# Second feed-forward product of eight encoder layers in three float32r passes instead of float32, with the token tensor parked in HBM meanwhile

## What is computed

```python
for i in range(8):
    residual = x
    Q = elu(x @ Wq[i] + bq[i]) + 1          # 16 heads of 64
    Kf = elu(x @ Wk[i] + bk[i]) + 1
    V = x @ Wv[i] + bv[i]
    ...
    y = gelu(att @ Wo[i] + bo[i])
    x = layer_norm(y + residual, ln1_s[i], ln1_b[i])
    residual = x
    h = gelu(x @ W1[i] + b1[i])             # 128 -> 512
    h = gelu(h @ W2[i] + b2[i])             # 512 -> 128: the product that is changed
    x = layer_norm(h + residual, ln2_s[i], ln2_b[i])
```

## Time and profile before

| what | us |
|---|---|
| median of 3 runs (lowest, highest) | 3317.26 (3315.12, 3319.06) |
| profiled execution, its own time | 3315.69 |
| span of that execution in the trace | 3313.6 |
| PE busy in the span | 2981.3 |
| DVE busy | 2659.7 |
| ACT busy | 2443.1 |
| POOL busy | 855.6 |

### The profile page before, as it was taken

The page is one execution under the profiler, slowest core; times in us unless marked ns, Lnnn a source line. Parts: engine busy times, 40 slices in busy tenths (PEclk is TensorE's granted clock), DMA queues, the critical chain, the costliest instruction groups (busy, mean ns, idle before and its releaser), DMA issues. The chain is left out here.

```text
span 3313.6 us, 50990 instructions
## 1 busy us (share of the span) xinstructions
PE 2981.3 (90%) x14368; PEld 1986.3 (60%) x14368; DVE 2659.7 (80%) x10476; ACT 2443.1 (74%) x4542; POOL 855.6 (26%) x1011
## 2 busy tenths in 40 slices
...
DMA packets 31561, 46.33 MB, mean 14 GB/s; under 512 B 5315, under 2 KB 21731, under 8 KB 31334
## 3 DMA queue, kind: packets, MB, share of 16 engines
...
...
## 5 line engine op out<-in xcount | busy, mean ns | idle before, releaser
L1836 DVE TENSOR_SCALAR t_feat_q<-t_recip,t_neg_mean 128x256 f32<-128x256 f32 x1024 | 399.9, 453 | 112.0 <-ACT t_recip L1701 109.4
L1549 PE MATMUL t_o_ps<-t_feat_q,t_wo 128*128 128x512 f32 x1024 | 471.9, 594 | 6.3 <-issue 3.6
L1693 ACT ACTIVATE t_recip<-t_feat_q,t_z_scale 128x256 f32<-128x256 f32 x1024 | 434.7, 499 | 1.7 <-DVE t_feat_q L1836 1.0
L1679 ACT ACTIVATE t_exp_k<-t_k_ps 128x1024 f32<-128x1024 f32 x256 | 259.7, 1014 | 231.4 <-PE t_k_ps L1526 231.4
L1799 DVE CUSTOM_DVE_ANT_0 t_junk<-t_v_ps,t_feat_k 128x256 f32<-128x256 f32 x1024 | 390.5, 419 | 7.7 <-PE t_v_ps L1526 7.3
L1948 POOL TENSOR_TENSOR t_var_eps<-t_moments,t_ln_eps 128x4 f32<-128x4 f32 x128 | 69.2, 540 | 1237.6 <-DVE t_moments L1847 1237.6
L1789 DVE SCALAR_TENSOR_TENSOR t_feat_k<-t_exp_k,t_k_ps 128x256 f32<-128x256 f32 x1024 | 369.2, 417 | 19.9 <-ACT t_exp_k L1679 19.8
L1683 ACT ACTIVATE t_exp_q<-t_q_ps 128x1024 f32<-128x1024 f32 x256 | 261.4, 1021 | 80.4 <-PE t_q_ps L1526 79.3
L1825 DVE SCALAR_TENSOR_TENSOR t_feat_q<-t_exp_q,t_q_ps 128x1024 f32<-128x1024 f32 x256 | 312.7, 1221 | 8.8
L1549 PEld LDWEIGHTS t_o_ps<-t_feat_q,t_wo 128*128 128x128 f32 x1024 | 194.1, 190 | 178.3 <-issue 158.4
L243 POOL TENSOR_TENSOR a_probs<-a_probs,a_inv 128x256 f32<-128x256 f32 (+1 forms) x256 | 208.9, 837 | 275.8 <-DVE a_inv L340 275.8
...
## 6 DMA issues: line engine op xcount, KB each, us to landing
t_raw_w<-in_wk SPq DMA_DIRECT2D x8, 512.0 KB, 3.8
t_raw_w<-in_wq SPq DMA_DIRECT2D x8, 512.0 KB, 4.7
t_raw_w<-in_wv SPq DMA_DIRECT2D x8, 512.0 KB, 5.6
t_raw_o<-in_wo SPq DMA_DIRECT2D x8, 512.0 KB, 3.6
t_raw<-in_w SPq DMA_DIRECT2D x16, 256.0 KB, 2.8
x<-in_x SPq DMA_DIRECT2D x4, 512.0 KB, 7.0
tokens_dram<-r_hn SPq DMA_DIRECT2D x8, 256.0 KB, 2.3
e_w_raw<-in_fc_w SPq DMA_DIRECT2D x4, 512.0 KB, 4.0
```

Source lines behind the costliest of these rows:

```text
L1549: last = pe.matmul(o_ps[:], wo[:, chunk, :], feat_q[:, s, chunk, :], start=(chunk == 0), stop=(chunk == NC - 1), skip_group_check=True)
L1679: act.activation(exp_k[:], k_ps[:], ACT.Exp, bias=-1.0).then_inc(c["k_exp"], 1)
L1693: last = act.activation(recip[:, q % 2, k * UNIT + n * SEQ:k * UNIT + (n + 1) * SEQ], feat_q[:, s, chunk, cols], ACT.Ln, bias=1.0, scale=z ...
L1836: last = dve.tensor_scalar(feat_q[:, s, chunk, cols], recip[:, q % 2, k * UNIT + n * SEQ:k * UNIT + (n + 1) * SEQ], -1.0, neg_mean[:, s, n ...
```

## The change

`second_feed_forward` becomes three float32r passes for each of its four chunks: twelve products of 128x128 by 128x512 in place of four float32 ones. Its weight is split by POOL once a layer (`swap_w2`, one more instruction and one more wait). Its input `hid` is split for every unit in two halves of 128x1024: ACT copies the high part (`hid_hi`), DVE subtracts it (`hid_lo`). PE starts when both high halves and the first low half are there, and waits for the second low half before its last two products. The first gelu of the next unit waits for the splits of the last.

To make room in SBUF, `x` is stored to HBM at the end of the entry phase (eight DMAs of 256 KB, as its parts become ready), `raw_o`, `raw_1`, `raw_2` and `hid` are laid into its place, and it is loaded back in two DMAs of 1 MB: the first half from SP once all weights are swapped, during the layers; the second half as the first DMA of `finish_phase`, where the fifth group of tiles (`join`) waits for it.

```diff
             def second_feed_forward(u, follows):
-                pe.wait_ge(c["hid_ready"], 4 * u + 5)
+                pe.wait_ge(c["hid_hi_ready"], 2 * u + 3)
+                pe.wait_ge(c["hid_split"], 2 * u + 2)
                 pe.wait_ge(c["w2_ready"], layer_of(u) + 2)
                 if follows:
                     pe.wait_ge(c["state_t_ready"], u - 1 + 2 + PER)
                 for j in range(NF):
-                    last = pe.matmul(m0[:], w2[:, j, :], hid[:, j, :], start=(j == 0), stop=(j == NF - 1))
+                    pe.matmul(m0[:], w2_hi[:, j, :], hid_hi[:, j, :], start=(j == 0), stop=False, skip_group_check=True)
+                    pe.matmul(m0[:], w2_lo[:, j, :], hid_hi[:, j, :], start=False, stop=False, skip_group_check=True)
+                for j in range(NF):
+                    if j == 2:
+                        pe.wait_ge(c["hid_split"], 2 * u + 3)
+                    last = pe.matmul(m0[:], w2_hi[:, j, :], hid_lo[:, j, :], start=False, stop=(j == NF - 1), skip_group_check=True)
                 last.then_inc(c["w2_filled"], 1)
...
             def first_gelu(u, j):
                 act.wait_ge(c["w1_filled"], 4 * u + j + 2)
+                if j == 0:
+                    act.wait_ge(c["hid_split"], 2 * u + 1)
                 act.activation(hid[:, j, :], (m1, m0)[j % 2][:], ACT.Gelu_apprx_tanh, bias=param(u, 1 + j)).then_inc(c["hid_ready"], 1)
+            def split_hid(u, h):
+                act.wait_ge(c["hid_ready"], 4 * u + 2 * h + 3)
+                if h == 0 and (not isinstance(u, int) or u >= 1):
+                    act.wait_ge(c["w2_filled"], u + 1)
+                act.activation(hid_hi[:, 2 * h:2 * h + 2, :], hid[:, 2 * h:2 * h + 2, :], ACT.Copy).then_inc(c["hid_hi_ready"], 1)
...
                 if Dn:
+                    split_hid(t - 3, 0)
                     first_gelu(t - 3, 2)
                     first_gelu(t - 3, 3)
...
                 if A:
                     exp_queries(t, 2)
+                if Dn:
+                    split_hid(t - 3, 1)
                 if E:
                     act.wait_ge(c["n2_turned"], t - 4 + 2)
...
+            def split_hid(u, h):
+                dve.wait_ge(c["hid_hi_ready"], 2 * u + h + 2)
+                dve.tensor_tensor(hid_lo[:, 2 * h:2 * h + 2, :], hid[:, 2 * h:2 * h + 2, :],
+                                  hid_hi[:, 2 * h:2 * h + 2, :].bitcast(F32), ALU.subtract).then_inc(c["hid_split"], 1)
...
                     feature_q(t, s, 1)
+                if Dn:
+                    split_hid(t - 3, 0)
                 if E:
                     layernorm_stats(t - 4, 1, m0, c["z2_turned"], c["bn2_done"], c["stats2_ready"])
...
                     layernorm_stats(t - 2, 0, m1, c["z1_turned"], c["bn1_done"], c["stats1_ready"])
+                if Dn:
+                    split_hid(t - 3, 1)
                 if A:
                     feature_q(t, s, 2)
                     values(t, s, 1, 1)
...
             def swap_w2(layer):
                 pool.wait_ge(c["raw_2_in"], 16 * layer + 17)
                 carry(2)
-                copy(w2[:], raw_2[:]).then_inc(c["w2_ready"], 1)
+                copy(w2_hi[:], raw_2).then_inc(c["w2_hi_ready"], 1)
+                pool.wait_ge(c["w2_hi_ready"], layer + 2)
+                pool.tensor_tensor(w2_lo[:], raw_2, w2_hi[:].bitcast(F32), ALU.subtract).then_inc(c["w2_ready"], 1)
...
+            for n in range(TURNS):
+                sp.wait_ge(c["x_added"], n + 1)
+                sp.dma_start(g["x_dram"][:, GT * n:GT * n + GT, :], g["x"][:, GT * n:GT * n + GT, :]).then_inc(c["x_stored"], 16)
             t = g["t_sems"]
             start_counters(sp, t.values())
...
             sp.wait_ge(c["const_in"], 32)
+            sp.wait_ge(c["x_stored"], 16 * TURNS)
...
-        raw_o = sb("t_raw_o", [P, NC, D])
-        raw_1 = sb("t_raw_1", [P, FF])
-        raw_2 = sb("t_raw_2", [P, NF, D])
+        raw_o = g["x"][:, 0:8, :]
+        raw_1 = g["x"][:, 8:12, :].rearrange("p a d -> p (a d)")
+        raw_2 = g["x"][:, 12:16, :]
...
-        hid = sb("t_hid", [P, NF, UNIT])
+        hid = g["x"][:, 16:32, :].rearrange("p (j a) d -> p j (a d)", j=NF)
...
+            sp.dma_start(g["x"][:, 0:16, :], g["x_dram"][:, 0:16, :]).then_inc(c["x_in"], 16)
+            sp.wait_ge(c["x_in"], 17)
...
         def _(sp):
+            sp.dma_start(g["x"][:, 16:32, :], g["x_dram"][:, 16:32, :]).then_inc(c["x_in"], 16)
             sp.dma_start(w_raw[:], d["w_mix"]).then_inc(c["w_in"], 16)
...
+                if GT * n == TILES // 2:
+                    dve.wait_ge(c["x_in"], 16)
                 dve.wait_ge(c["turned_back"], n + 1)
```

More of the change, by code:

```diff
@@ L1197, in first_layer_tiles @@
              "ln_ready recip_ready att_ready o_filled y1_ready z1_ready z1_turned bn1_done stats1_ready var1_ready rstd1_ready "
[1 row of a table removed]
[1 row of a table added]
              "bn2_done stats2_ready var2_ready rstd2_ready n2_ready n2_turned state_t_ready x_hi_ready x_split "
[1 row of a table removed]
-             "raw_w_in raw_b_in raw_o_in raw_1_in raw_2_in").split()
[1 row of a table added]
+             "raw_w_in raw_b_in raw_o_in raw_1_in raw_2_in x_in").split()
     g["t_sems"] = {n: sem("t_" + n) for n in names}
@@ L1227, in combine_and_entry_phase @@
         names = ("ones_made zeroed diag_ready gate_filled term_ready x_added bn_done stats_ready var_ready rstd_ready xn_ready "
-                 "x_turned state_ready w_in b_in const_in hi_ready lo_ready bias_ready").split()
+                 "x_turned state_ready x_stored w_in b_in const_in hi_ready lo_ready bias_ready").split()
         c = {n: sem("n_" + n) for n in names}
@@ L1394, in stack_phase @@
         w1_lo = sb("t_w1_lo", [P, FF], F32R)
-        w2 = sb("t_w2", [P, NF, D])
+        w2_hi = sb("t_w2_hi", [P, NF, D], F32R)
+        w2_lo = sb("t_w2_lo", [P, NF, D], F32R)
         x_hi = sb("t_x_hi", [P, 2, UNIT], F32R)
@@ L1416, in stack_phase @@
         x1_lo = sb("t_x1_lo", [P, UNIT], F32R)
-        hid = sb("t_hid", [P, NF, UNIT])
+        hid = g["x"][:, 16:32, :].rearrange("p (j a) d -> p j (a d)", j=NF)
+        hid_hi = sb("t_hid_hi", [P, NF, UNIT], F32R)
+        hid_lo = sb("t_hid_lo", [P, NF, UNIT], F32R)
         y2 = sb("t_y2", [P, UNIT])
```

18 lines of the change are left out of this document (11 added, 7 removed), and 4 rows, old and new, of the table names.

## The result

The changed kernel takes **3404.98 us** (median of 4 runs, 3401.24 to 3407.71); the kernel before, run beside it, 3317.08 (3315.12 to 3319.06). The ratio is 1.0264, 95% interval 1.0248 to 1.0281: slower, by 88 us where the forecast had 77. The profiled execution took 3407.03 us with a span of 3405.0.

What follows compares the result with a forecast made beforehand. A step was taken as a chain through ACT, DVE and PE, with PE nearly full; 3315.7 + 75.6 (61 x 1.24) + 2 = 3393.3 us, and with the runs' median 1.6 us higher, 3394 us; 8 in 10 range 3350 to 3445.

Steps and rivals of the forecast that it cites:

- Two branches that meet in `biases(3)`: At PE's biases(3), the product's branch (PE, ACT) comes 0.36 us later, DVE's 1.24; the step grows by 1.24 us.
- the DVE branch: DVE's list from the statistics to feature_k(2): 2.15 us later with 0.91 us to spare, so +1.24 us and last.
- ACT's first copy on the ring, its second free: First copy, before the gelus, delays them and z2 by 1.0 us; second fills the 1.11 us wait ahead of state_t.
- the ring: Chain through ACT, DVE and PE that closes once a step, at 35.19 us a step before the change.
- DVE's first subtraction free, its second in full: First fills DVE's wait for z2 and costs nothing; second, ahead of feature_q(2), adds its whole 1.15 us.
- What DVE gets back from POOL: attention(1) starts just past the end of POOL's t_x_lo and falls from 1.97 to 1.14 us, regaining 0.83 us.
- PE's saving: Second feed-forward product on PE falls from 3.54 to 2.9 us, 0.64 us a unit, which turns into a wait.
- Storing x nothing, loading it 2 us: Storing x before the layers costs nothing; loading its second half ahead of the mixture's weights costs 2 us once, ends 0 and 5.
- "Once a layer ... nothing": POOL's one more subtraction per layer for the weight split, some 1.3 us, costs nothing, as POOL has time.
- the step's term: 61 steps with both keys and feed-forward, each 1.24 us longer: 75.6 us in the layers.

Runs made afterwards that it cites:

- e2: Changed kernel without DVE's second subtraction and the last two of the product's twelve passes; 3355.54 us (one run), 35.80 us a step.
- e2b: Changed kernel without DVE's second subtraction and the product's last two passes, POOL's low part of the next input held until attention(1) is done; 3316.01 us (one run).
- e3: Changed kernel without ACT's first copy, DVE's first subtraction and two low passes, first two gelus writing float32r; 3343.52 us (one run).
- e4: Kernel before, with POOL's low part of the next input held until DVE has finished attention(1); 3307.28 us, ratio 0.9969.
- e7: Kernel before with only x stored to HBM, loaded back and its place used; product stays float32, no splits; 3321.11 us, ratio 1.0013.
- e1: Changed kernel with one wait more a layer: POOL starts the weight swap only after attention(1); 3393.58 us, ratio to before 1.0233.
- e8: Changed kernel without any split of the hidden values: gelu writes float32r, product is eight passes; 3286.35 us (one run), 34.85 us a step.
- e8b: Changed kernel without any split of the hidden values, eight passes, POOL's low part of the next input held until attention(1) is done; 3254.72 us (one run).
- e5: Changed kernel with all input splits on POOL in quarters, its low part of the next input held until attention(1) is done; 3331.34 us, ratio 1.0045.

## Why the prediction held, and where a term was off

Point by point, against its own steps:

- **Two branches that meet in `biases(3)`; the DVE branch becomes last: right.** PE waits 0.41 us for DVE there, and the step is 1.17 to 1.18 us longer where the forecast had 1.24. With the delay measured in e2, 0.94 us, and the second subtraction at 1.14, the forecast's sum gives 0.94 + 1.14 − 0.91 = 1.17. e2b and e3 take the two parts of it away one at a time and find 35.22 and 35.42, where its terms give 35.3 and 35.4.
- **ACT's first copy on the ring, its second free: right.** `z2` waits 0.94 us; the wait ahead of `state_t` is filled.
- **DVE's first subtraction free, its second in full: right.** e2b against the changed kernel: 1.14 us, against 1.15.
- **What DVE gets back from POOL: right in a regular step**, shown by e2 and e4: the 1.97 us are the collision. It was as narrow as the prediction said: `attention(1)` starts 0.10 us behind the end of POOL's low part, at 1856.57 and 1856.47, where the forecast had 0.12.
- **PE's saving: right in size** (0.66 us measured, 0.64 forecast), and it lies in a wait, so that it did not count.
- **Storing x nothing, loading it 2 us: right.** The layers start at the same time (837.57 us, before 837.87); the finish is 2.6 us longer; e7, with only this, +3.9 us.
- **"Once a layer ... nothing": this term was off.** Beyond the 1.18 us of every step the seven swap steps measured 6.6 us: 0.5 us each from the collision (3.6), and 1.5 us for each of two falls of the clock more than before (3). The forecast looked at what waits for POOL's swap and not at whom the swap blocks; it priced `attention(1)` from one regular step, though the swap step of the kernel before already had 3.43 us at that place.
- **The two loop returns had no term in the forecast.** They measured 5.5 us beyond the 1.18 each: 2.2 us of longer waits, and a fall of the clock behind each.

In sum: 61 x 1.18 = 72 us (forecast 75.6), the nine long steps 12.1 (0), the last four intervals 94.75 − 93.63 = 1.1 (0), the finish 2.6 (2). That is 88 of the 91 us between the two spans. Of the rest 2.7 lie before the first `state_t`, where the clock after the change shows 0.66 from 966 to 971 us, and 1.00 before it.

So the mechanism held, and the step's term is 72 of the 91 us. That the whole came within 11 us of the forecast is partly luck: the step was priced 3.6 us too high over all steps, which hid a part of the 17 us that had no term or too small a one.

## What to carry to other kernels

When two branches meet, their slack can be spent once: price an edit on each branch from the meeting point, and don't add a piece's cost alone to the other's. An instruction moved or added on POOL has two prices, the work that waits for it and the DVE instructions that it runs beside; look for the second in every kind of step, the once-a-layer ones too. In three places here one wait on POOL, which has time, took such a collision away (e1, e4, and 0.57 us a step from e8 to e8b).

## What the runs showed beyond that

A subtraction of 128x512 on POOL held up a 128x16 multiplication on DVE for 1.08 us (e5), and in the other direction DVE's second subtraction stretched POOL's 128x4 addition from 0.56 us (its row in the kernel before, and in e2) to 1.09. That a wait of PE with the same length, 1.48 us, is followed by 3.4 us of lowered clock in some swap steps and by none in others was not expected. The two falls more in the swap steps cost 3 of the 12 us that the forecast lacked, and the two behind the longer waits of the loop returns about as much.
